# A two-layer graph attention kernel on Trainium2: three engines' loops over the batches of the second layer written out

## The reference

```python
h = jnp.maximum(_layernorm(x, axis=-1), 0.0)
q = (h @ W).reshape(B, N, H, D)
e_src = jnp.einsum('bnhd,d->bnh', q, a_src)
e_dst = jnp.einsum('bnhd,d->bnh', q, a_dst)
e = e_src[:, :, None, :] + e_dst[:, None, :, :]
e = jnp.where(e >= 0, e, 0.2 * e)
e = jnp.where(mask, e, -9e15)
attn = jax.nn.softmax(e, axis=2)
x = x + jax.nn.elu(jnp.einsum('bijh,bjhd->bihd', attn, q).reshape(B, N, H * D))
```

## Time and profile before

| | us |
|---|---|
| median of 3 runs | 5143.4 |
| lowest and highest | 5140.66, 5144.62 |
| the profiled execution, its own time | 5128.5 |
| its span, first to last instruction | 5126.7 |
| TensorE, VectorE, ScalarE busy | 4799.6, 3755.8, 2899.6 |

### The profile page before, as it was taken

One profiled execution on the slowest core, in us unless ns is written; L12 is line 12 of the kernel. 1 busy time (PEld: TensorE's weight loads), 2 busy tenths in 40 slices (PEclk: granted clock), 3 DMA queues, 4 the chain that ended last, 5 costly groups with the idle time before them and its releaser, 6 DMA issues. The chain is left out here.

```text
span 5126.7 us, 139194 instructions
## 1 busy us (share of the span) xinstructions
PE 4799.6 (94%) x56352; PEld 4402.8 (86%) x56352; DVE 3755.8 (73%) x7147; ACT 2899.6 (57%) x3121; POOL 1412.9 (28%) x1661
## 2 busy tenths in 40 slices
PE   6999999999999999999999999956988988989899
PEld 4998899889898899889988989855988988989899
DVE  6666667666676667666766666647888888898898
ACT  4444444444444444444444444426877877888787
POOL 3343344334343344334433433330000000000000
PEclk9999999999999999999999999978999999999999
DMA  5000100010001010010001000022111121121210
GB/s 205 17 18 17 30 26 18 22 26 26 22 18 26 18 30 18 17 30 26 18 22 26 26 18 13 22 82 68 42 60 63 38 69 55 44 75 37 66 63 28
DMA packets 110193, 198.02 MB, mean 39 GB/s; under 512 B 7088, under 2 KB 93488, under 8 KB 103088
## 3 DMA queue, kind: packets, MB, share of 16 engines
q1 hardware_dynamic: 98464, 144.80, 8.4%
q0 software_dynamic: 11024, 43.53, 3.3%
HBM read 112.53 MB, written 38.03 MB: 29 GB/s over the span
## 5 line engine op out<-in xcount | busy, mean ns | idle before, releaser
L577 PEld LDWEIGHTS outs<-v_s,probs 128*128 128x128 f32 x16384 | 1977.1, 192 | 111.6 <-issue 27.6
L690 ACT ACTIVATE slot<-slot,shift 128x1024 f32<-128x1024 f32 x1024 | 1111.6, 1088 | 1586.7 <-PE slot L567 1586.7
L577 PE MATMUL outs<-v_s,probs 128*128 128x128 f32 x16384 | 1991.5, 275 | 5.0 <-DVE ctx_part L847 5.0
L831 DVE SCALAR_TENSOR_TENSOR probs<-slot,bound 128x1024 f32<-128x1024 f32 x1024 | 1250.7, 1224 | 708.1 <-ACT slot L690 707.6
L1391 ACT ACTIVATE cond<-s_all,d_sign 128x1024 bf16<-128x1024 f32 x1024 | 1123.9, 1142 | 218.5 <-DVE u L1546 213.0
L566 PE MATMUL slot<-q_hl,k_hl 128*128 128x512 f32 x2048 | 894.4, 437 | 41.5 <-DVE probs L831 27.0
L393 POOL TENSOR_TENSOR ctx_sum<-ctx_sum,ctx_part 128x256 f32<-128x256 f32 x896 | 650.1, 731 | 1017.5 <-DVE ctx_part L847 1017.1
L1292 PE MATMUL sums<-x_mixed,u 128*128 128x130 f16 x8192 | 811.9, 223 | 18.6 <-issue 18.6
L1546 DVE TENSOR_TENSOR u<-cond,mask 128x1024 f16<-128x1024 bf16 x1024 | 690.9, 681 | 179.6 <-PE sums L1296 105.2
L567 PE MATMUL slot<-q_hl,k_hl 128*128 128x512 f32 x2048 | 804.1, 393 | 0.0
L1296 PE MATMUL sums<-x_mixed,mask 128*128 128x65 f16 x8192 | 782.0, 196 | 0.0
(11 more groups left out here) (137 smaller groups left out, 3663.4 us busy)
## 6 DMA issues: line engine op xcount, KB each, us to landing
q_hl<-q_hl POOLq DMA_DIRECT2D x128, 256.0 KB, 3.7
s_all<-s_turned SPq DMA_DIRECT2D x32, 1024.0 KB, 5.1
xs<-in_x SPq DMA_DIRECT2D x32, 512.0 KB, 4.4
x<-y SPq DMA_DIRECT2D x32, 512.0 KB, 3.1
x_s<-x SPq DMA_DIRECT2D x32, 512.0 KB, 5.8
o_s<-x SPq DMA_DIRECT2D x16, 1024.0 KB, 6.3
out<-o_s SPq DMA_DIRECT2D x16, 1024.0 KB, 4.7
probs<-in_adj SPq DMA_DIRECT2D x11, 1024.0 KB, 5.1
```

Of the source, the lines that this page charges most:

```text
L577: end = nc.tensor.matmul(outs[i % OUTS][:, q, :], probs[:, i % PROBS, r, q * P:(q + 1) * P], v_s[:, c * JC + r, h * E1:h * E1 + P], start= ...
L690: nc.scalar.activation(slot[:, :, :], slot[:, :, :], ACT.Exp, bias=shift[:, 0:1], scale=SCALE).then_inc(act_done, 1)
L831: nc.vector.scalar_tensor_tensor(probs[:, i % PROBS, :, :], spot(kind, "step", s, i)[:, :, :], P_LOW, bound[:, (i // H) % 2, :, :], ALU.ma ...
```

## The change

In the second layer the loops of TensorE, ScalarE and VectorE become Python loops: the seven and twice six iterations are written out one behind the other, with constants in place of registers.

```diff
-            with pe.Fori(0, B - 1) as b:
+            for b in range(B - 1):
                 batch(b, False)
             batch(B - 1, True)
...
-            with act.Fori(1, B - 1) as b:
+            for b in range(1, B - 1):
                 batch(b, False, False)
...
-            with dve.Fori(1, B - 1) as b:
+            for b in range(1, B - 1):
                 batch(b, False, False)
```

## The result

The changed kernel took 5071.9 us (median of four runs, 5068.1 to 5080.2) against 5142.0 for the kernel before (four runs, 5140.5 to 5144.6): a ratio of 0.9868, 95% interval 0.9853 to 0.9884, so 70.2 us gained where 57.4 were forecast. The profiled execution of the changed kernel is the slowest of its four: 5080.2 us, span 5078.4, 48.3 less than that of the kernel before.

What follows compares the result with a forecast made beforehand. Stalls where the second layer's loops jump back between batches were taken to bound the kernel: 200.9 - 143.5 = 57.4 us gained, registers and longer code 0, so 5143.4 - 57.4 = 5086 us (78%), range 5067 to 5104.

Steps and rivals of the forecast that it cites:

- The seams: Second layer, six batch changes where loops jump back: 200.94 us would become 22.80 us each, 64.1 us gained.
- The second rival: Second-layer batch changes: stalls come from what all six batches do at their start, such as loads; time stays 5143 us; 4%.
- The clock: Second layer: stretches at half clock make each new batch change 23.92 us, gain 57.4 us, ends 48.9 and 74.2.
- the forecast's other end: Second layer: all units concerned run at full clock, 74.2 us gained, 5069 us; 7% as a rival.
- Registers, longer code: Second layer: dropping register instructions before waits gains nothing, and fetching longer straight code costs nothing; both taken as 0.
- the fourth rival: Inside second-layer batches: straight code runs dry, 24 waits of 3.5 us lose 84 us, 5170 us; 3%.
- From the profile to the median: Whole kernel: median 14.9 us above the profiled execution, taken to lie outside the seams; 5143.4 - 57.4 = 5086 us.
- The range: Whole kernel: 5067 to 5104 us, leaving out near 2 in 10.
- the first rival: Second-layer batch changes: the wait moves to VectorE, each stays at 28.70 us, 28.7 us gained, 5115 us; 8%.

## Why the prediction was right, and where it was off

**The seams.** Right: six seams at 24.2 to 24.4 us, no TensorE wait without a releaser in the first profile of the changed kernel. The step that carried it was to compare the one seam where the loops fall through with the six where they jump. That it was the jump taken, and not registers, branch or the next batch's loads, was argued then. The branch rows show it: 5.0 to 6.0 us taken, 0.08 us not taken, with two packets of code in between. The second rival falls with the result itself, since the loads are all still there and the seams are short. So does the sum by the Trainium skill's page "Advanced Engine Details and Errata" (Control Flow Timing), about 108 ns for a compare-and-branch: the trace has 83 ns for TensorE's where it falls through, but 4973 to 5977 ns for the six that are taken, and the measurement decides.

**The clock.** Right in kind, with 24.29 us for a seam where 23.92 was taken. In both profiles of the changed kernel and in that of the kernel with ScalarE's loop all the seams, 21 of 21, have a stretch at the lower clock, not six of eight. With loops of one iteration two of six ran at full clock, and with the first layer written out too three of seven, which is toward the forecast's other end.

**Registers, longer code.** Right, at 0 to within the rows. Units 3 to 5 of batches 1 to 6, at full clock throughout, sum to 439.5 us with register waits and to 439.9 with constants. At the first seam of the kernel with TensorE alone written out, ScalarE and VectorE enter their loops with registers and without a jump, and it takes 24.37 us. A few waits without a releaser did appear on TensorE in the straight code: none in the first profile of the changed kernel, two of 0.9 us together in its second, both inside batches, and three of 2.6 us together (the longest 1.4, two of them at a seam) with the first layer written out too. That is small against the 84 us of the fourth rival, but it isn't nothing; that it is code coming late is not shown.

**From the profile to the median.** This is the step that was off. The forecast took the 14.9 us between the profiled execution and the median "to lie outside the seams" and carried 57.4 us over unchanged. The second profile of the kernel before shows the opposite: of its 12.2 us more, 7.3 are in the six seams and 8.7 in units at the lower clock, less 4.9 before batch 0 was through. An execution like the median one had 208 us of seams, by which the seams' term is 208.2 - 6 x 24.29 = 62.5 us.

**How near the sum came.** In part by luck, since two misses of opposite sign are in it. From profile to profile the gain was 48.3 us, 9.1 less than the 57.4 forecast: 2.2 for the seams (55.2) and 6.9 given back elsewhere in the layer, most of it in units at the lower clock. From there to the medians it was 21.9 us more (70.2), since the kernel before was profiled in an execution 13.5 us below its median of four and the changed kernel in one 8.4 above its own. The difference, 12.8 us, is what the forecast was short of the medians. The second profiles, each close to its kernel's median on its chip, have 5138.9 and 5071.4 us, 67.5 apart: 62.5 in the six seams and 10.2 in the units 1, 6 and 7 of batches 1 to 6, less 4.6 before the first seam. They are from two chips; on the one where the kernel before took 5123.7, the gain by medians is 52. The changed kernel took 5072 both times.

**The range.** Its upper bound, 5104 us, is called a third of the way to the first rival. From 5086 to 5115 it is nearer two thirds; the other description, a seam that keeps 1.6 us on top of 5094.5, gives it.

**The first rival** (VectorE's standstill stays) was a real cost with the right price: 28.0 to 28.7 us for each seam where VectorE and ScalarE jump, 27.8 to 28.6 where VectorE alone does. It didn't come since the change takes that jump too.

## What to carry to other kernels

Compare a loop's seams with the one where it ends: that one runs through without a jump, and the difference is about what writing it out is worth (64.1 us by the one clean seam here, 55.2 to 62.5 measured, since that seam ran at full clock and the new ones mostly did not). Costs of several engines at one seam overlap, so that an edit of the engine with the smaller one shows nothing until the larger is gone; and an engine that runs ahead by some buffers may need no edit, as ScalarE here. Look at what is still running when the branch is issued: matmuls already issued hid most of the jump in the first layer, and 0.6 us of them hid little in the second. Before carrying a gain from one profiled execution to the median of the runs, take a second profile.

## What the runs showed of the hardware

- A jump back of TensorE cost a seam 9 to 11 us here: mostly 5.0 to 5.5 us idle until the first matmul, 2.8 to 4.1 us more a step later, and a stretch at 1.2 GHz that made 32 matmuls of 1.17 us take 1.94. VectorE's cost some 4 us, ScalarE's nothing.
- A compare-and-branch of TensorE lasted 0.08 us not taken and 5.0 to 6.0 us taken in the second layer of the kernel before, and 3.9 to 4.6 us taken in its first, of which the matmuls issued before it covered all but 0.3 us at the seam shown.
- Taken branches show in the count of instruction packets: 19 to 22 fewer of 16 KB without TensorE's six (478 to 480 against 458 or 459), 40 fewer of 8 KB without the other engines' ten.
- A wait of 2.08 us in an otherwise busy TensorE was mostly followed by a stretch at half clock, worth 1.6 us of a unit; in the kernel where the longest such wait from batch 1 on was 1.57 us none followed in the seams and units 7. The exception was, for one, unit 7 of batch 4 in the kernel before, which has such a wait (2.1 us) and a clock of 1.00.
- The price of a jump varied from run to run and between chips (seams of 28.7 to 35.5 us in one and the same kernel), while the changed kernel had medians of 5071.9 and 5071.7 us. SyncE's loads and stores of 1 MB fall into the same stretches (DMA share 0.27 to 0.39 in the earlier trace rows); whether they delay the fetch was not tried. The two packets of q8 at the seam of batch 6 took 1.6 and 1.7 us, the three at the seventh seam, 3 to 5 us apart, 0.9 to 1.2.
